# Attention values with 16 products a unit instead of 24, their halves added by an accumulating transfer

## The chip, the cores and the metric

One core of a Trainium2 chip runs the whole kernel. TensorE multiplies from the on-chip memory into eight accumulator banks (`psum`), VectorE and ScalarE read and write both, GpSimd reads and writes the on-chip memory only, and SyncE (SP) issues transfers. Each engine works through its own list in order; engines wait for one another by semaphores. The metric is the device time of one execution in microseconds (us), smaller is better, as the median over several executions.

## The reference

An adapter projection, attention, a second adapter projection and a mixture-of-experts layer over 32 sequences of 64 tokens and 1024 columns, all in 32-bit floats:

```python
x = x + attn(cond(x, labeler, W, lora_A, lora_B), w_qkv, b_qkv, w_o, b_o)
x = x + ffn(cond2(x, language, W, Wr, A, B), W_base, b_base, W_router, A, B)
...
q, k = apply_rope(q, 0), apply_rope(k, 0)          # 32 query heads, 8 key/value heads of 32
scores = where(causal, q @ k.T / sqrt(32), -1e20)
out = softmax(scores) @ v
```

## The kernel before

The kernel has five stages, one behind the other on every engine: it folds the first projection into the query/key/value weights, runs attention, folds the second projection into the last weights, then the output projection, then the mixture of experts. Precision is kept by splitting each operand into a rounded high part and a low rest and adding three products, high by high, high by low and low by high.

Attention goes over 16 units of 128 tokens, two sequences (`b` = 0, 1) each. It is a pipeline of steps over `u`, written out by hand (`steps`): a step projects unit `u`, does the scores and the softmax of unit `v = u - 1`, and the values of unit `w = u - 2`. Steps 2 to 14 are one loop body, step 15 is the same body written out; steps 0 and 1 have no values yet, step 16 has scores and values but no projection (there TensorE does the first products of the next fold, `fold2.first(k)`, in its place), and step 17 has only the last values (`last_values`).

TensorE's order within a step is set by the table `BESIDE`. The projection of a unit is cut into 8 slices `k` of 3 parts each (L912), and `(k, part): [...]` names the work that stands ahead of that part. That work is: `transpose_p` (L959), the transposition of the probabilities of one `b`; `attend` (L974), the value products of one `b`; `transpose_qk` (L931), the transposition of rotated queries and keys in three turns; `scores` (L944). At the end of the step stand the transposition of the adapter's small product (`transpose_down`, L985) and the four products `up` (L991) that finish the projection. `BESIDE_FIRST` is the table of step 1.

In `attend` the contraction runs over two heads by 64 keys, so the values stand in blocks on a diagonal: `vb_h` and `vb_l` are 128 rows by 4 x 32 columns of which half are zero. For each `b` there are 3 pairs (`vb_h` by `pt_h`, `vb_l` by `pt_h`, `vb_h` by `pt_l`) by 2 quads by 2 halves `j`, 12 products of 256 moving columns, all into the bank `s_ps[:, b]`.

VectorE per step: the low part of the probabilities (`probs_low`, L749), four multiplications of the rotation (`rotate`, L744), the low part of the values (L797), the low parts of queries and keys (L753, L816), `less_max` for each `b` (mask L834, maximum L836, subtraction L838), `inverse` (L771), `low_down` (L778), `sum_up` (L764), the low part of `lows` (L856) for which `up` waits, and the read-out of the projection (L867). ScalarE takes the high parts, reads out the values (`values_out`, L605), and forms the exponentials (L617 for `b` = 0 in 16 pieces with their sums, L619 for `b` = 1). GpSimd does the two additions of the rotation (L711, L713), the low parts of x (`split_x`, L694) and the division by the sum (`normalise`, L704). SP loads x and adapter rows and stores each unit's values into a scratch tensor (L562).

## Time and profile before

| | |
|---|---|
| median of 3 executions | 1154.16 us (1153.38 to 1154.23) |
| the profiled execution, its time | 1153.42 us |
| its span, first to last instruction | 1151.3 us |
| TensorE busy in the span | 1132.6 us, 98% |
| VectorE, ScalarE, GpSimd busy | 684.9, 409.2 and 202.8 us |
| share of TensorE in the chain that ended last | 87% |
| share of VectorE and ScalarE in that chain | 7% and 4% |

The span is what the hardware profiler saw; the execution's own time has 2.1 us more around it. Busy time of an engine is the union of its instructions; matmuls are pipelined, so a busy TensorE need not be at its peak. The chain that ended last is followed back from the last instruction, at each step to what released it.

### The profile page before, as it was taken

The numbers are of one execution on the slowest core, as the hardware profiler recorded it, in microseconds if no ns is written. First come the engines' busy times: TensorE is split into PE (matmuls) and PEld (weight loads), VectorE is DVE, ScalarE is ACT, GpSimd is POOL, SyncE is SP. The second block draws the span as 40 slices with busy tenths as digits, with TensorE's granted clock in tenths as the row PEclk, the third lists the DMA queues.
The fourth block names the chain that finished last, engine by engine and source line by source line (L and its number), as shares of the span: only waits on it lengthen the run. The fifth ranks groups of instructions, "written<-read, shape, count | busy, mean of one in ns | idle before, by whom it ended". The sixth has DMA issues, their size and how long they took to land.

```text
span 1151.3 us, 16982 instructions
## 1 busy us (share of the span) xinstructions
PE 1132.6 (98%) x6176; PEld 992.3 (86%) x6176; DVE 684.9 (59%) x1201; ACT 409.2 (36%) x1172; POOL 202.8 (18%) x131
## 2 busy tenths in 40 slices
PE   8999999999999999999989999999999999999998
PEld 6888888999999999999889998888888888888887
DVE  5312137878887888888894234233136766666664
ACT  5312124555555555555553234111123322222221
POOL 0000124443334433334351001000000000000000
PEclk9999999999999999999999999999999999999999
DMA  8020032111111111110042115473561323332222
GB/s 287 18 66 19 10 113 73 46 46 52 58 46 46 46 54 46 46 46 36 19 169 92 57 38 165 128 217 101 158 183 43 123 110 110 111 110 96 75 69 92
DMA packets 90082, 98.29 MB, mean 85 GB/s; under 512 B 7730, under 2 KB 74162, under 8 KB 90034
## 3 DMA queue, kind: packets, MB, share of 16 engines
q1 hardware_dynamic: 89890, 97.37, 26.2%
q8 instruction: 32, 0.52, 0.2%
q10 hardware_dynamic: 144, 0.26, 0.1%
q14 instruction: 16, 0.13, 0.0%
HBM read 72.45 MB, written 25.17 MB: 85 GB/s over the span
## 4 chain that ended last, share of the span: by engine, by line
PE 87%; DVE 7%; ACT 4%; DMA 1%; issue 0%; POOL 0%; DVEq 0%; SPq 0%
PE psum L912 18%; PE psum L1563 15%; PE psum L1871 14%; PE psum L280 13%; PE psum L1291 8%; PE psum L1851 4%; PE psum L974 4%; PE psum L1949 4%; ACT prob L617 3%; PE psum L944 3%; PE psum L959 2%; PE psum L931 1%; PE psum L991 1%; DVE prob L838 1%; DVE smax L836 1%; DVE prob L834 1%
## 5 line engine op out<-in xcount | busy, mean ns | idle before, releaser
L912 PE MATMUL psum<-p_h,c_high_low 128*128 128x512 f32 (+1 forms) x768 | 194.3, 360 | 0.5 <-DVE qkv L867 0.5
L912 PEld LDWEIGHTS psum<-p_h,c_high_low 128*128 128x128 f32 x768 | 133.2, 188 | 14.2 <-issue 0.7
L280 PE MATMUL psum<-c_high_low,w_h 128*128 128x512 f32 x384 | 119.5, 396 | 5.7 <-ACT c_high_low L215 5.7
L1563 PE MATMUL psum<-ring,rows 128*128 128x512 f32 x528 | 123.7, 392 | 1.0 <-DVE t_plain L1265 0.8
L1563 PEld LDWEIGHTS psum<-ring,rows 128*128 128x128 f32 x528 | 98.8, 188 | 23.9 <-DVE t_plain L1265 2.3
L1291 PE MATMUL psum<-chunk,rows 128*128 128x384 f32 (+1 forms) x576 | 108.7, 343 | 1.2 <-DVE qkv L867 0.7
L912 PE MATMUL psum<-p_l,c_high_low 128*128 128x512 f32 (+1 forms) x384 | 104.2, 366 | 0.0
L1291 PEld LDWEIGHTS psum<-chunk,rows 128*128 128x128 f32 x576 | 101.8, 190 | 2.0 <-DVE qkv L867 1.0
L280 PEld LDWEIGHTS psum<-c_high_low,w_h 128*128 128x128 f32 x384 | 73.4, 191 | 22.4 <-ACT c_high_low L215 5.7
L704 POOL TENSOR_TENSOR prob<-prob,sinv 128x1024 f32<-128x1024 f32 x32 | 61.1, 1908 | 126.7 <-DVE sinv L771 126.7
L694 POOL TENSOR_TENSOR c_high_low<-ring_plain,c_high_low 128x512 fp32r<-128x512 f32 x32 | 41.4, 1293 | 235.0 <-PE psum L280 139.1
L617 ACT ACTIVATE prob<-prob 128x64 f32<-128x64 f32 x240 | 57.8, 242 | 67.7 <-DVE prob L838 67.7
L912 PE MATMUL psum<-end_h,c_high_low 128*128 128x320 f32 x256 | 75.9, 309 | 0.0
L280 PE MATMUL psum<-c_high_low,w_l 128*128 128x512 f32 x192 | 73.9, 391 | 0.0
L912 PEld LDWEIGHTS psum<-p_l,c_high_low 128*128 128x128 f32 x384 | 66.0, 189 | 6.3
L1871 PE MATMUL psum<-t_high,s_blocks 128*128 128x512 f32 x192 | 64.6, 398 | 0.0
L266 DVE TENSOR_TENSOR p_l<-psum,p_h 128x512 fp32r<-128x512 f32 (+1 forms) x24 | 14.2, 602 | 83.1 <-ACT p_h L254 42.3
L1523 DVE TENSOR_TENSOR ring<-ring_plain,ring 128x512 fp32r<-128x512 f32 x22 | 15.2, 691 | 75.3 <-ACT ring L1518 75.3
L1563 PE MATMUL psum<-at,rows 128*128 128x512 f32 x240 | 56.5, 391 | 0.0
L912 PEld LDWEIGHTS psum<-end_h,c_high_low 128*128 128x128 f32 x256 | 47.5, 188 | 7.9
L1563 PEld LDWEIGHTS psum<-at,rows 128*128 128x128 f32 x240 | 45.0, 188 | 9.9
L1851 PE MATMUL psum<-gates,a_blocks 128*128 128x272 f32 x384 | 50.3, 290 | 0.0
(172 smaller groups left out, 2225.1 us busy)
## 6 DMA issues: line engine op xcount, KB each, us to landing
ring_plain<-in_x_t SPq DMA_DIRECT2D x32, 256.0 KB, 2.6
attn_scratch<-ring_plain SPq DMA_DIRECT2D x16, 512.0 KB, 2.6
ring_plain<-attn_scratch SPq DMA_DIRECT2D x32, 256.0 KB, 4.0
raw<-x_t_scratch SPq DMA_DIRECT2D x16, 512.0 KB, 4.1
rest<-in_b_base SPq DMA_DIRECT2D x16, 512.0 KB, 4.2
out<-rest SPq DMA_DIRECT2D x15, 512.0 KB, 2.7
ring_plain<-in_wqkv_t SPq DMA_DIRECT2D x10, 512.0 KB, 6.1
a_raw<-in_lora_a SPq DMA_DIRECT2D x32, 128.0 KB, 2.1
```

What stands on the lines that cost most here:

```text
L280: mm = pe.matmul(to, stationary, moving, start=k == 0 and m == 0, stop=k == KT - 1 and last, skip_group_check=True)
L617: last = act.activation(prob[:, 0, g, c, :], prob[:, 0, g, c, :], ACT.Exp, scale=SCALE, accum_out=ssum[:, 0, g, c:c + 1])
L694: pool.tensor_tensor(x_l[:, ks(half), :], x_raw[:, ks(half), :], x_h[:, ks(half), :].bitcast(F32), ALU.subtract).then_inc(x_low, 1)
L704: pool.tensor_tensor(rows, rows, sinv[:, b, :, :].rearrange("p g c -> p (g c)").unsqueeze(2).to_broadcast([P, 2 * KVH, SEQ]), ALU.mult).th ...
L912: mm = pe.matmul(to, sx[:, kk, :], moving(w, n, kk), start=first, stop=False, skip_group_check=True)
L944: mm = pe.matmul(o, qq[:, b, cols, :].rearrange("p g t -> p (g t)"), kk[:, q, b, :, :].rearrange("p c t -> p (c t)"), start=n == 0, stop=n ...
L974: mm = pe.matmul(s_ps[:, b, q * 4 * SEQ:(q + 1) * 4 * SEQ], vv[:, b, q, j, :, :].rearrange("p c d -> p (c d)"), pp[:, q, j, :, :].rearrang ...
L1291: mm = pe.matmul(self.tile(n, width), stationary, moving, start=k == 0 and m == 0, stop=k == KT - 1 and m == 2, skip_group_check=True)
L1563: mm = pe.matmul(self.psum[:, self.BANK_OF[i], :], w[:, cols], s, start=m == 0 and p == 0, stop=m == KT - 1 and p == 2, skip_group_check=True)
L1851: mm = pe.matmul(self.gate_ps[:, u, :], s[:, k % HALF, :], self.room.gates[:, m, k, :], start=k == 0 and n == 0, stop=k == KT - 1 and n == ...
L1871: mm = pe.matmul(self.banks[self.BANK_OF[name]], s[:, k, :], w[:, k, :], start=name in ("p1", "p5", "p6") and k == 0 and n == 0, stop=k == ...
L1949: mm = pe.matmul(self.banks[{"c11": "a", "c12": "c", "c21": "b", "c22": "d"}[name]], self.zt[:, r, s, u, :], w[m], start=name == "c22" and ...
```

## The change

Five things change. First, high and low values stand side by side in one tensor `vb`, each as 2 x 32 columns; one product with 128 stationary columns gives high by high in the upper 64 rows of the result and low by high in the lower 64, and the product with the low probabilities has 64 stationary columns. That is 8 products for each `b` in place of 12. A result of one `b` is now twice as large and lies in two banks (by quad, no longer by `b`), so the second `attend` waits until ScalarE has read out the first (`pv_out`), and ScalarE reads out in two copies each time.

Second, the upper and lower 64 rows have to be added. They lie on different partitions; GpSimd issues two transfers a unit that add the lower rows onto the upper (`add_low_values`), behind `split_x` of the first half and ahead of `normalise`. SP waits for both (`pv_summed`) and stores two halves.

Third, GpSimd's rotation waits for all four multiplications (`rot_re` and `rot_im`) before its first addition. Fourth, VectorE's low part of the values moves behind `probs_low` of the second `b`. Fifth, entries of `BESIDE` move: the transpositions of queries and keys from (2, 1) and (3, 1) to (3, 0) and (3, 2), the scores from (4, 0) and (5, 0) to (4, 2) and (5, 2). At the end of attention SP's loads for the next fold are arranged around the later last store.

```diff
-    vb_h, vb_l = (sb(n, [P, BPU, QUADS, 2, 4, HD], F32R) for n in ("vb_h", "vb_l"))
+    vb = sb("vb", [P, BPU, QUADS, 2, 2, 2, HD], F32R)
+    values = ring[:, 2, :], sb("values_odd", [P, D])
...
+            if value and not score:
+                sp.wait_ge(s_done, 2 * UNITS)
+                fold2.load_lora(sp)
+                sp.wait_ge(fold2.row_low, fold2.STAGED)
+                fold2.load_chunk(sp, 1, 0)
             if value:
-                sp.wait_ge(pv_out, 2 * w + 2)
-                sp.dma_start(a["attn"][bass.ds(w, 1), :, :].rearrange("o p c -> (o p) c"),
-                             attn[:, :, :, :].rearrange("p k b t -> p (k b t)")).then_inc(stored, 16)
+                sp.wait_ge(pv_summed, 32 * w + 32)
+                for j in range(2):
+                    sp.dma_start(a["attn"][bass.ds(w, 1), j * SEQ:(j + 1) * SEQ, :].rearrange("o p c -> (o p) c"),
+                                 values[j][high_rows, :]).then_inc(stored, 16)
...
             if b == 0:
-                need(act, stored, 16 * w)
-            act.activation(attn[:, :, b, :], s_ps[:, b, :].rearrange("p (k t) -> p k t", k=KT), ACT.Copy).then_inc(pv_out, 1)
+                need(act, stored, 32 * w)
+            for j in range(2):
+                to = values[j].rearrange("p (k b t) -> p k b t", k=KT, b=BPU)[:, :, b, :].rearrange("p (q g) t -> p q g t", q=QUADS)
+                cols = s_ps[:, :, j * GRP * SEQ:(j + 1) * GRP * SEQ].rearrange("p q (g t) -> p q g t", g=GRP)
+                last = act.activation(to, cols, ACT.Copy)
+            last.then_inc(pv_out, 1)
...
+        def add_low_values():
+            for j in range(2):
+                pool.dma_start(values[j][high_rows, :], values[j][low_rows, :], accum_op=ALU.add).then_inc(pv_summed, 16)
+
...
                 pool.wait_ge(rot_re, v + 1)
+                pool.wait_ge(rot_im, v + 1)
                 pool.tensor_tensor(roped[:, :, :, 0], roped[:, :, :, 0], rot_t[:, 0, :, :], ALU.subtract).then_inc(rotated, 1)
-                pool.wait_ge(rot_im, v + 1)
                 pool.tensor_tensor(roped[:, :, :, 1], roped[:, :, :, 1], rot_t[:, 1, :, :], ALU.add).then_inc(rotated, 1)
+            if value:
+                pool.wait_ge(pv_out, 2 * w + 2)
...
+            if value:
+                add_low_values()
             if score:
                 normalise(v, 0)
...
-            n = 0
-            for vv, pp in ((vb_h, pt_h), (vb_l, pt_h), (vb_h, pt_l)):
+            else:
+                pe.wait_ge(pv_out, 2 * v + 1)
+            for parts, pp in ((2, pt_h), (1, pt_l)):
...
-                        mm = pe.matmul(s_ps[:, b, q * 4 * SEQ:(q + 1) * 4 * SEQ], vv[:, b, q, j, :, :].rearrange("p c d -> p (c d)"),
-                                       pp[:, q, j, :, :].rearrange("p g t -> p (g t)"), start=n == 0, stop=pp is pt_l and j == 1, skip_group_check=True)
-                        n += 1
+                        v_at = vb[:, b, q, j, 0:parts, :, :].rearrange("p m h d -> p (m h d)")
+                        mm = pe.matmul(s_ps[0:parts * SEQ, q, j * GRP * SEQ:(j + 1) * GRP * SEQ], v_at, pp[:, q, j, :, :].rearrange("p g t -> p (g t)"),
+                                       start=parts == 2 and j == 0, stop=parts == 1 and j == 1, skip_group_check=True)
...
-                  (2, 1): [(attend, 2, 1), (transpose_qk, 1, (0, 1))], (3, 1): [(transpose_qk, 1, (2,))],
-                  (4, 0): [(scores, 1, 0)], (5, 0): [(scores, 1, 1)]}
+                  (2, 1): [(attend, 2, 1)], (3, 0): [(transpose_qk, 1, (0, 1))], (3, 2): [(transpose_qk, 1, (2,))],
+                  (4, 2): [(scores, 1, 0)], (5, 2): [(scores, 1, 1)]}
```

TensorE, loop body, from the second `attend` to the first turns of `transpose_qk`. Each row is a line, an operation, output and inputs and the shape; `x3` is three of a kind. Before:

```order
L974 MATMUL psum<-pt_h,vb_h 128x256 [waits pt_high]
L974 MATMUL psum<-pt_h,vb_h 128x256 x3
L974 MATMUL psum<-pt_h,vb_l 128x256 x4
L974 MATMUL psum<-pt_l,vb_h 128x256 [waits pt_low]
L974 MATMUL psum<-pt_l,vb_h 128x256 x3
L931 MATMUL psum<-ident,roped 128x128 [waits pt_low,rotated]
L931 MATMUL psum<-ident,roped 128x128 x7
L912 MATMUL psum<-p_l,c_high_low 128x512 x2
L912 MATMUL psum<-p_l,c_high_low 128x256
L912 MATMUL psum<-end_l,c_high_low 128x320
L912 MATMUL psum<-p_h,c_high_low 128x512 x2
```

The same place in the changed kernel, where `attend` is L995, the projection L931 and `transpose_qk` L950:

```order
L995 MATMUL psum<-pt_h,vb 128x256 [waits pv_out,pt_high]
L995 MATMUL psum<-pt_h,vb 128x256 x3
L995 MATMUL psum<-pt_l,vb 64x256 [waits pt_low]
L995 MATMUL psum<-pt_l,vb 64x256 x3
L931 MATMUL psum<-p_l,c_high_low 128x512 x2
L931 MATMUL psum<-p_l,c_high_low 128x256
L931 MATMUL psum<-end_l,c_high_low 128x320
L931 MATMUL psum<-p_h,c_high_low 128x512 x2
L931 MATMUL psum<-p_h,c_high_low 128x256
L931 MATMUL psum<-end_h,c_high_low 128x320
L950 MATMUL psum<-ident,roped 128x128 [waits pt_low,rotated]
```

The second `attend` has 8 products for 12, waits for `pv_out`, and is followed by two parts of the projection before the eight transpositions, which followed it at once.

TensorE, loop body, ahead of the first score product (L944). Before, from the last transposition of `transpose_qk` to the scores:

```order
L931 MATMUL psum<-ident,roped 128x128
L912 MATMUL psum<-p_l,c_high_low 128x512 x2
L912 MATMUL psum<-p_l,c_high_low 128x256
L912 MATMUL psum<-end_l,c_high_low 128x320
L912 MATMUL psum<-p_h,c_high_low 128x512 x2
L912 MATMUL psum<-p_h,c_high_low 128x256
L912 MATMUL psum<-end_h,c_high_low 128x320
L944 MATMUL psum<-k_h,q_h 128x256 [waits pv_out,k_low,qk_low]
```

In the changed kernel, where the scores are L963:

```order
L950 MATMUL psum<-ident,roped 128x128
L931 MATMUL psum<-p_h,c_high_low 128x512 x2
L931 MATMUL psum<-p_h,c_high_low 128x256
L931 MATMUL psum<-end_h,c_high_low 128x320
L931 MATMUL psum<-p_h,c_high_low 128x512 [waits x_low]
L931 MATMUL psum<-p_h,c_high_low 128x512
L931 MATMUL psum<-p_h,c_high_low 128x256
L931 MATMUL psum<-end_h,c_high_low 128x320
L931 MATMUL psum<-p_l,c_high_low 128x512 x2
L931 MATMUL psum<-p_l,c_high_low 128x256
L931 MATMUL psum<-end_l,c_high_low 128x320
L963 MATMUL psum<-k_h,q_h 128x256 [waits pv_out,k_low,qk_low]
```

Between the third turn and the scores there stood two parts of the projection (a part is one product each for the columns 2 x 512, 256 and 320), now three. Ahead of the third turn stood three behind the first two turns, now two, and two more stand ahead of these. So five parts lay between the second `attend` and the scores, and now seven.

GpSimd, loop body. Before:

```order
L711 TENSOR_TENSOR roped<-roped,rot_t 128x640 [waits rot_re]
L713 TENSOR_TENSOR roped<-roped,rot_t 128x640 [waits rot_im]
L694 TENSOR_TENSOR c_high_low<-ring_plain,c_high_low 128x512 [waits x_high]
L704 TENSOR_TENSOR prob<-prob,sinv 128x1024 [waits s_inv]
L698 TENSOR_TENSOR end_l<-a_raw,end_h 128x2x8x32 [waits a_high]
L694 TENSOR_TENSOR c_high_low<-ring_plain,c_high_low 128x512 [waits x_high]
```

In the changed kernel (`split_x` L705, the transfers L720, `normalise` L715):

```order
L727 TENSOR_TENSOR roped<-roped,rot_t 128x640 [waits rot_im,rot_re]
L728 TENSOR_TENSOR roped<-roped,rot_t 128x640
L730 ISA
L704 ISA [waits pv_out]
L705 TENSOR_TENSOR c_high_low<-ring_plain,c_high_low 128x512 [waits x_high]
L720 DMA ring_plain<-ring_plain 64x1024
L720 DMA values_odd<-values_odd 64x1024
L713 ISA
L715 TENSOR_TENSOR prob<-prob,sinv 128x1024 [waits s_inv]
```

The rotation's first addition waits for both multiplication pairs, and two transfers stand between `split_x` and `normalise`.

## Rows read from the trace of the kernel before

**Rows 1.** Windows, one loop step: length, busy PE PEld DVE ACT POOL, clock, DMA.

```profile
439.40:466.60 27.20, 27.15 (x177) 24.67 (x176) 22.44 (x34) 14.64 (x54) 11.36 (x8) 1.00 0.14 48
```

**Rows 2.** Chain that ended last, 438 to 468 us: start, us, what.

```profile
442.61 1.43 PE psum L974 x12
...
447.83 1.50 PE psum L974 x12
...
450.21 2.19 PE psum L912 x12
...
454.07 1.45 PE psum L944 x12
...
459.31 3.95 ACT prob L617 x32
```

**Rows 3.** Weight-load queue, timeline of the same step: start, us.

```profile
464.25 0.14 PEld L985 LDWEIGHTS psum<-ident,low 128*128 128x128 f32 x1
...
465.84 0.77 PEld L991 LDWEIGHTS psum<-pb,lows 128*128 128x128 f32 x4 [0.37 <-DVE lows L856]
```

**Rows 4.** Waits over the whole run: us, times, longest.

```profile
PEld psum L991 <- DVE lows L856: 5.6, 15, 0.5
```

**Rows 5.** TensorE, timeline of the same step.

```profile
439.39 1.04 PE L959 MATMUL psum<-ident,prob 128*128 128x128 f32 x8
...
449.17 1.04 PE L931 MATMUL psum<-ident,roped 128*128 128x128 f32 x8
...
453.90 0.28 PE L944 MATMUL psum<-k_h,q_h 128*128 128x256 f32 x1
...
457.53 0.27 PE L944 MATMUL psum<-k_h,q_h 128*128 128x256 f32 x1
...
466.64 0.60 PE L959 MATMUL psum<-ident,prob 128*128 128x128 f32 x4
```

**Rows 6.** VectorE, timeline of the same step.

```profile
444.13 0.82 DVE L744 TENSOR_TENSOR roped<-qkv,sin 128x640 f32<-128x640 f32 x1
444.87 2.21 DVE L744 TENSOR_TENSOR rot_t<-qkv,cos 128x640 f32<-128x640 f32 x1
...
453.24 0.41 DVE L753 TENSOR_TENSOR q_l<-psum,q_h 128x256 fp32r<-128x256 f32 x1
...
455.54 1.23 DVE L834 TENSOR_TENSOR prob<-psum,hidden 128x1024 f32<-128x1024 f32 x1 [1.06 <-PE psum L944]
...
463.46 0.59 DVE L778 TENSOR_SCALAR low<-psum 64x128 f32<-64x128 f32 x2
464.24 1.22 DVE L764 TENSOR_REDUCE ssum<-prob 128x16 f32<-128x1024 f32 x1 [0.19 <-ACT prob L619]
465.50 0.29 DVE L856 TENSOR_TENSOR lows<-psum,lows 32x128 fp32r<-32x128 f32 x1
```

**Rows 7.** ScalarE, timeline of the same step.

```profile
449.37 0.60 ACT L605 ACTIVATE ring_plain<-psum 128x512 f32<-128x512 f32 x1 [3.40 <-PE psum L974]
449.87 0.38 ACT L648 ACTIVATE keys<-psum 128x256 f32<-128x256 f32 x1
```

**Rows 8.** GpSimd, timeline of the same step.

```profile
454.93 1.29 POOL L694 TENSOR_TENSOR c_high_low<-ring_plain,c_high_low 128x512 fp32r<-128x512 f32 x1 [6.05 <-ACT c_high_low L582]
463.62 1.91 POOL L704 TENSOR_TENSOR prob<-prob,sinv 128x1024 f32<-128x1024 f32 x1 [7.41 <-DVE sinv L771]
```

**Rows 9.** Transfers to the scratch: issue and landing.

```profile
L562 SPq DMA_DIRECT2D attn_scratch<-ring_plain x16: 344/355/374, 204.8 to 618.5; - x16
...
DMA to landing us min/median/max: 2.6/2.9/6.3
```

**Rows 10.** TensorE, timeline of the last scoring step.

```profile
587.33 1.04 PE L931 MATMUL psum<-ident,roped 128*128 128x128 f32 x8
588.22 2.40 PE L1291 MATMUL psum<-chunk,rows 128*128 128x392 f32 x12
...
606.28 1.21 PE L959 MATMUL psum<-ident,prob 128*128 128x128 f32 x8 [2.01 <-POOL prob L704]
```

40 lines of the change are left out of this document (18 added, 22 removed).

## The prediction

> **What bounds the kernel now.** I read the windows of one step of the attention loop first. Of 27.20 us TensorE is busy 27.15, at full granted clock [rows 1]. That reads as a stage bound by TensorE, in which every product taken away is time won. The chain that ended last says otherwise. In each step it leaves TensorE after the score products and runs over VectorE and ScalarE: 3.95 us of it are the exponentials of the first batch [rows 2]. The weight-load queue shows where that chain comes back: the load ahead of the `up` products stood idle 0.37 us for L856 [rows 3]. The reader is to see that this happens in every step, 15 times and 5.6 us in all [rows 4]. So two limits lie 0.37 us apart: TensorE's own work, 27.25 - 0.37 = 26.88 us a step, and a loop through the softmax.
>
> I take the step's zero at its first transposition, 439.39; the next one begins at 466.64, so the step is 27.25 us. The first score product starts at 453.90, which is 14.51 after zero, and the next step begins 12.74 us after that [rows 5]. The second number is the length of the tail, and it is fixed by data: scores end, L834 starts at 455.54, three operations a batch, ScalarE's exponentials from 459.31 [rows 2], then `low_down` (L778) at 463.46, the sum L764 at 464.24, which waited for ScalarE's second exponential, and L856 at 465.50 [rows 6]. L856 lets `up` go, and `up` ends the step. TensorE's order is fixed, so the first number is pure TensorE work ahead of the scores. A step costs "TensorE work ahead of the scores" + 12.74, or TensorE's whole work, whichever is more.
>
> **The change, part by part.**
> *Products.* 24 become 16. The two groups of 12 take 1.43 and 1.50 us [rows 2], 0.119 a product, and the extra 0.07 of the second is a pause ahead of its third group for `pt_low`, which the new order on VectorE brings earlier. Eight of the new products have 64 stationary columns instead of 128. No row shows such a product. All keep 256 moving columns; the nearest row is the score products with 256 moving columns, 12 in 1.45 us, 0.121 each [rows 2]. Bounds: 0.12 and nothing. I take 0.12, because the two kinds of product in the chain with 256 moving columns cost the same. Then a group is 8 x 0.119 = 0.95, and a step's work falls by 1.43 + 1.50 - 1.90 = 1.03 us. All of it lies ahead of the scores.
> *The table.* The order above shows that the scores now stand behind two more parts of the projection. Three parts, 12 products, take 2.19 us [rows 2], so 0.73 each, and the gap from first to second scores agrees: 457.53 - 453.90 = 3.63 [rows 5], less 1.45 for the scores, is 2.18 for three. Two parts are 1.46. The first score product starts at 14.51 - 1.03 + 1.46 = 14.94.
> *Are its inputs ready by then?* The transpositions of queries and keys started at 449.17, 9.78 [rows 5], and now stand at 9.78 - 1.03 + 1.46 = 10.21. The last of the data the scores need is L753, done at 453.24 + 0.41, which is 4.48 after those transpositions [rows 6]. That gives 14.69, before 14.94. ScalarE's two copies of the values, instead of one, add one more copy of 0.50 (from 449.37 to 449.87 [rows 7]) at about 9.5; ScalarE is free again at about 10.0 and the keys are due at 10.8, so this is covered by 0.8. GpSimd's rotation starts after all four multiplications. The fourth took 2.21 us beside 0.82 for the third, since GpSimd's first rotation ran [rows 6]; now all four take 0.74 each (the distance from the start of the third, 444.13, to that of the fourth, so the first starts at 3.3) and end at 6.2. GpSimd's split of 512 columns takes 1.29 [rows 8], a rotation of 640 so some 1.6, and two end at 9.4, before 10.21. What is won, 1.4 us of VectorE, lies where VectorE waits anyway: zero. If this cover fails, each 0.1 us late is 0.1 a step.
> *Tail.* Neither VectorE's order behind the scores nor ScalarE's is touched, so 12.74 stays. `low_down` ends at 463.46 + 0.59 = 24.66 now and 25.09 then, while TensorE comes to the transposition that needs it (464.25, 24.86 now [rows 3]) at 23.83. It waits 1.3 us there, and some 0.5 at `up`. The step is 14.94 + 12.74 = 27.68 us: 0.43 longer, although it holds 1.03 us less work.
> *The accumulating transfers.* Two are issued on GpSimd behind the split of the first half, which ends at 454.93 + 1.29 = 16.83 and ahead of `normalise`, due at 463.62 (24.23) now [rows 8] and 24.66 then. So 7.8 us are free for two issues, and 1.1 more until the next step's transposition. The trace has no transfer issued by GpSimd. Bounds for one issue: SP's 0.35 us [rows 9] below, and above, for want of any such row, what the cover and the slack hold, 4.45. I take it as hidden. The Trainium skill (SBUF — State Buffer, section "A bandwidth-pool intuition that's wrong (but worth ruling out)") says a transfer issued from GpSimd that takes some 0.62 us alone takes 3.1 beside a VectorE copy that holds the shared port; two of these would be 6.2, an estimate, and still inside the cover. No row here shows it. The landing, 2.9 us for a store now [rows 9], comes twice in series, add and store, so 5.8 us behind the issue; even from 24.7 that ends at 30.5, and the next reading-out of values, which waits for it, is due at 27.7 + 4.2. SP waits for the add in front of its store, and behind that queues the load of x for the step after next, which is not read within the next 17 us.
> *Second reading-out.* The second group now waits for ScalarE to empty the banks. The first group ended at 442.61 + 1.43 = 444.04 [rows 2], 4.65, and ends at 4.2 then; two copies of 0.5 and the passing of the signals bring it to 5.5; the second group started at 447.83, 8.44, and starts at 7.9: covered by 2.4.
> *Count.* The loop and the step unrolled behind it are steps 2 to 15, 14 in all: 14 x 0.43 = +6.0. Steps 0 and 1 have no value products and their own table, untouched.
> *The last scoring step* has no projection. There the transpositions (587.33) moved behind the 12 fold products that follow them (588.22, 2.24 without the pipelined end), and the third turn has no cover left [rows 10]. If VectorE's other work absorbs it all the loss is 0; if it is passed on whole, it is some 3.3 us of later scores. TensorE waits 2.01 us for `normalise` at 606.28 [rows 10], so the chain is tight and I pass on 2.3. The two last groups save 1.0. Net +1.3, ends -1 and +4.
>
> Sum: 1153.42 (span 1151.3 + 2.1 around it) + 6.0 + 1.3 = 1160.7. The median of before is 0.7 above its profiled execution; I say 1161, 0.6% slower. An error of 0.2 us in the 14.94 is 2.8 us, so its own range is 1157 to 1166.
>
> **Rivals.**
> *A. TensorE is the bound after all, faster.* 27.15 of 27.20 busy speaks for it. Then 16 x 1.03 = 16.5 us go and the time is 1153.4 - 16.5 + 1.3 = 1138. It needs a tail shorter than 12.74 - 0.43 = 12.31 before anything is won, and under 10.9 for all. Against: the wait of [rows 4] is there in every step, and no operation of the tail is stretched by GpSimd.
> *B. The narrow products are cheap, no change.* If eight of them cost half, 0.06, the scores start at 14.47 and the step is 27.21: 1153.4 - 0.6 + 1.3 = 1154. From 0.04 downwards it would be faster. Against: the price follows the moving columns in both rows I have. The Trainium skill (TensorE: Matmul & The Clock Gate, section "LDWEIGHTS (loading the stationary operand)") has the load go with its columns, 107 ns for 128 and 53 for 64; were the load what spaces these products, 0.053 each would be about this case, an estimate. The trace cannot say which side spaces them.
> *C. GpSimd's issues gate `normalise`, slower still.* At 5 us each they run 10 - 8.9 = 1.1 us over a step, 14 x 1.1 = 15 more: 1176. It decides from 4.45 us each. For it: no row bounds such an issue from above. Against: nothing else is on GpSimd in that stretch [rows 8], and its next work starts 7.4 us behind the split.
>
> **How the numbers follow.** Forecast 0.72, A 0.10, B 0.08, C 0.10. A measurement of this kernel can tell 0.2%, 2.3 us. Slower is forecast and C, 0.82; same is B, 0.08; faster is A, 0.10. The range 1155 to 1170 holds the forecast, the upper part of B and the lower part of C, and leaves A out.
>
> **What would show it.** Right: a step of 27.7 us; TensorE idle some 1.3 us at the `low` transposition behind VectorE's `low_down` and 0.5 at `up`; 16 products a step at 0.12; score products 14.9 after the step's first transposition; `normalise` still let go by `sinv`. Wrong: a step of 26 us (A), narrow products under 0.06 (B), `normalise` behind a long issue (C), or scores that wait for `q_l`, which would lengthen the step further.

## The result, and the profile after

The changed kernel takes 1163.04 us in the median of 4 runs (1161.78 to 1163.94), the kernel before 1154.15 beside it: 8.9 us more, ratio 1.0079 with a 95% interval of 1.0067 to 1.009. Forecast were 1161 and a range of 1155 to 1170.

The profiled execution took 1163.2 us, its span is 1161.4. From the page, the busy time of each engine:

```profile
PE 1120.1 (96%) x6048; PEld 975.4 (84%) x6048; DVE 670.8 (58%) x1201; ACT 422.4 (36%) x1204; POOL 218.1 (19%) x162
```

TensorE is busy 12.5 us less than before, and the kernel ends later: where TensorE had products to do, it now waits. Windows of one loop step, as [rows 1]:

```profile
443.80:471.40 27.60, 26.29 (x169) 23.57 (x168) 21.56 (x34) 15.49 (x56) 12.40 (x10) 1.00 0.30 67
```

Of 27.60 us TensorE is now idle 1.3, where it was idle 0.05. Its timeline, as [rows 5], says where:

```profile
441.33 0.30 PE L1005 MATMUL psum<-ident,low 128*128 128x128 f32 x1 [1.13 <-DVE low L796]
...
442.97 0.96 PE L1011 MATMUL psum<-pb,lows 128*128 128x512 f32 x4 [0.18 <-DVE lows L875]
443.77 1.03 PE L978 MATMUL psum<-ident,prob 128*128 128x128 f32 x8
...
446.83 0.64 PE L995 MATMUL psum<-pt_h,vb 128*128 128x256 f32 x4
447.31 0.63 PE L995 MATMUL psum<-pt_l,vb 128*64 128x256 f32 x4
447.78 1.03 PE L978 MATMUL psum<-ident,prob 128*128 128x128 f32 x8
...
453.95 1.03 PE L950 MATMUL psum<-ident,roped 128*128 128x128 f32 x8
...
458.70 0.28 PE L963 MATMUL psum<-k_h,q_h 128*128 128x256 f32 x1
...
471.44 1.03 PE L978 MATMUL psum<-ident,prob 128*128 128x128 f32 x8
```

The step begins at 443.77; the first score product comes 14.93 us later (14.51 before, 14.94 forecast). The next step begins at 471.44, which is 12.74 after that. The first exponentials of two steps, in ScalarE's timeline, lie 27.67 apart.

```profile
436.45 0.26 ACT L628 ACTIVATE prob<-prob 128x64 f32<-128x64 f32 x1 [4.73 <-DVE prob L857]
...
464.12 0.26 ACT L628 ACTIVATE prob<-prob 128x64 f32<-128x64 f32 x1 [4.73 <-DVE prob L857]
```

The forecast was 27.68. A value group (the products of one `attend`) goes from 446.83 to 447.78, 0.95 us for eight products; its four narrow ones take 0.47 as its four wide ones do. The waits over the whole run show that both idle pieces come 15 times. The lines of PE are TensorE's own, that of PEld is the weight-load queue's, as in [rows 4]:

```profile
PE psum L1005 <- DVE low L796: 17.6, 15, 1.8
...
PEld psum L1011 <- DVE lows L875: 7.5, 15, 0.6
...
PE psum L1011 <- DVE lows L875: 2.8, 15, 0.2
```

GpSimd's timeline shows the rotation that waits for all four multiplications, the two transfers, and what `normalise` waits for:

```profile
450.21 1.60 POOL L727 TENSOR_TENSOR roped<-roped,rot_t 128x640 f32<-128x640 f32 x1 [3.20 <-DVE rot_t L762]
451.76 1.77 POOL L728 TENSOR_TENSOR roped<-roped,rot_t 128x640 f32<-128x640 f32 x1
...
460.70 0.82 POOL L720 DMA_DIRECT2D ring_plain<-ring_plain  x1
461.27 1.09 POOL L720 DMA_DIRECT2D values_odd<-values_odd  x1
468.43 1.90 POOL L715 TENSOR_TENSOR prob<-prob,sinv 128x1024 f32<-128x1024 f32 x1 [6.07 <-DVE sinv L789]
```

An issue takes 0.82 or 1.09 us, and 6 us of idle time follow them. The rotation is done at 453.53, 0.4 before the transpositions at 453.95.

### The profile page after: what moved, and what is told of

Its sections match the earlier page's. It is cut to its first block, busy times and chain, and to the rows that moved or that the text cites. A ratio compares the mean times of both kernels' runs of the same rounds, so it can differ in the third digit from the quotient of the medians.

```text
span 1161.4 us, 16875 instructions
## 1 busy us (share of the span) xinstructions
PE 1120.1 (96%) x6048; PEld 975.4 (84%) x6048; DVE 670.8 (58%) x1201; ACT 422.4 (36%) x1204; POOL 218.1 (19%) x162
## 4 chain that ended last, share of the span: by engine, by line
PE 82%; DVE 10%; ACT 7%; DMA 1%; issue 0%; POOL 0%; DVEq 0%; SPq 0%
PE psum L931 15%; PE psum L1580 15%; PE psum L1888 13%; PE psum L280 12%; PE psum L1311 8%; ACT prob L628 5%; PE psum L1868 4%; PE psum L1966 4%; PE psum L995 2%; PE psum L978 2%; PE psum L963 2%; DVE ssum L782 2%; DVE prob L857 2%; DVE smax L855 2%; DVE prob L853 2%; PE psum L950 1%
## 5 line engine op out<-in xcount | busy, mean ns | idle before, releaser
L931 PE MATMUL psum<-p_h,c_high_low 128*128 128x512 f32 (+1 forms) x768 | 196.3, 363 | 0.5 <-DVE qkv L886 0.5
L931 PEld LDWEIGHTS psum<-p_h,c_high_low 128*128 128x128 f32 x768 | 132.0, 189 | 14.6 <-issue 0.7
L931 PE MATMUL psum<-p_l,c_high_low 128*128 128x512 f32 (+1 forms) x384 | 102.1, 361 | 0.0
L705 POOL TENSOR_TENSOR c_high_low<-ring_plain,c_high_low 128x512 fp32r<-128x512 f32 x32 | 41.4, 1293 | 235.1 <-PE psum L280 139.7
L715 POOL TENSOR_TENSOR prob<-prob,sinv 128x1024 f32<-128x1024 f32 x32 | 60.9, 1902 | 99.5 <-DVE sinv L789 99.5
L931 PE MATMUL psum<-end_h,c_high_low 128*128 128x320 f32 x256 | 76.1, 309 | 0.0
L931 PEld LDWEIGHTS psum<-p_l,c_high_low 128*128 128x128 f32 x384 | 67.2, 190 | 6.3
L771 DVE TENSOR_TENSOR q_l<-psum,q_h 128x256 fp32r<-128x256 f32 (+1 forms) x48 | 24.5, 511 | 53.4 <-ACT q_h L606 52.3
L931 PEld LDWEIGHTS psum<-end_h,c_high_low 128*128 128x128 f32 x256 | 47.4, 188 | 7.8
```

The lines of the kernel that those rows point to most:

```text
L705: pool.tensor_tensor(x_l[:, ks(half), :], x_raw[:, ks(half), :], x_h[:, ks(half), :].bitcast(F32), ALU.subtract).then_inc(x_low, 1)
L715: pool.tensor_tensor(rows, rows, sinv[:, b, :, :].rearrange("p g c -> p (g c)").unsqueeze(2).to_broadcast([P, 2 * KVH, SEQ]), ALU.mult).th ...
L771: dve.tensor_tensor(q_l[:, :, n0:n1, :].rearrange("p b n t -> p n b t"), q_ps(turn, at, n1 - n0), q_h[:, :, n0:n1, :].bitcast(F32).rearran ...
L931: mm = pe.matmul(to, sx[:, kk, :], moving(w, n, kk), start=first, stop=False, skip_group_check=True)
```

## The experiments

The steps turned out to be a ring: each turn begins with an instruction that waits for the end of the turn before. The table gives its three pieces in each trace: from VectorE's read-out of the projection (L867 before, L886 after) to the first transposition of rotated queries, from there to the first score product, from there to the next read-out. All are differences of starts in the timelines of one step. Each ratio is to the kernel before as it ran beside that kernel (medians from 1153.58 to 1154.15 us).

| kernel | read-out to transposition | to scores | to next read-out | step | median, us | ratio to before, interval |
|---|---|---|---|---|---|---|
| before | 10.05 | 4.73 | 12.48 | 27.26 | | |
| changed | 10.45 | 4.75 | 12.47 | 27.67 | 1163.04 | 1.0079, 1.0067 to 1.009 |
| e1 old table | 10.06 | 4.80 | 12.47 | 27.33 | 1155.3 | 1.0014, 1.0004 to 1.0024 |
| e2 before, table alone | 11.54 | 4.76 | 12.46 | 28.76 | 1176.54 | 1.0195, 1.0178 to 1.0212 |
| e3 no addition | 10.45 | 4.76 | 12.46 | 27.67 | 1163.37 | 1.008, 1.0063 to 1.0096 |
| e4 tail | 10.22 | 4.79 | 12.34 | 27.35 | 1157.89 | 1.004, 1.0026 to 1.0055 |
| e5 last table | 10.44 | 4.76 | 12.46 | 27.66 | 1159.96 | 1.005, 1.0033 to 1.0067 |
| e6 before, tail | 10.17 | 4.73 | 12.93 | 27.83 | 1161.46 | 1.0068, 1.0051 to 1.0085 |
| e7 early and tail | 10.18 | 4.54 | 13.02 | 27.74 | 1161.35 | 1.0067, 1.0051 to 1.0084 |
| e8 rotation early | 10.50 | 4.48 | 13.03 | 28.01 | 1164.16 | 1.0089, 1.0072 to 1.0106 |
| e9 one part | 10.07 | 4.54 | 12.55 | 27.16 | 1153.0 | 0.9991, 0.9982 to 1.0 |
| e10 before, wait alone | 9.97 | 4.80 | 12.46 | 27.23 | 1152.77 | 0.9991, 0.9982 to 1.0 |
| e11 split rotation | 10.81 | 5.03 | 12.56 | 28.40 | 1169.26 | 1.013, 1.0115 to 1.0146 |
| e12 low v early | 9.96 | 4.53 | 12.57 | 27.06 | 1151.93 | 0.9985, 0.9976 to 0.9994 |

**Which part costs.** e1 gives the changed kernel the old table back, e2 gives the kernel before the new table and nothing else, e3 takes the accumulating transfers out.

```diff
-                  (2, 1): [(attend, 2, 1)], (3, 0): [(transpose_qk, 1, (0, 1))], (3, 2): [(transpose_qk, 1, (2,))],
-                  (4, 2): [(scores, 1, 0)], (5, 2): [(scores, 1, 1)]}
+                  (2, 1): [(attend, 2, 1), (transpose_qk, 1, (0, 1))], (3, 1): [(transpose_qk, 1, (2,))],
+                  (4, 0): [(scores, 1, 0)], (5, 0): [(scores, 1, 1)]}
```

That is e1; e2 is the same the other way round. e3:

```diff
-                sp.wait_ge(pv_summed, 32 * w + 32)
+                sp.wait_ge(pv_out, 2 * w + 2)
...
-            if value:
-                add_low_values()
```

> The changed kernel with the table BESIDE of before; products, reading-out, transfers and rotation stay changed. Theory (the step is TensorE's order ahead of the scores + 12.74 us): the transpositions of queries and keys now stand 8.75 us after the step's start but their input, GpSimd's rotation, is done at 9.76 (451.76 + 1.77 in the trace of the changed kernel, step start 443.77), so TensorE waits 1.0 us for it; from there to the scores 4.73 us as before, so scores at 14.5 and a step of 27.3 against 27.67: 14 x 0.4 = 5.6 us less than the changed kernel, plus 2 to 3 us in the last scoring step, so about 1155. Rival (the longer step comes from the doubled reading-out, the transfers or the rotation, not from the table): no change against the changed kernel, 1163, or slower by the added wait, 1177.

> The kernel of before with only the table moved: 24 products, no transfers. TensorE has the same work in another order. Theory: each of the two parts that now stand ahead of the scores adds its 0.73 us to every step from 2 to 15, so scores at 15.97, a step of 28.71, 14 x 1.46 = 20.4 us more, and some 3 to 5 us in the last scoring step: 1154 + 24 = 1178. Rival (TensorE's total work is the bound, order does not matter): 1154 to 1156.

> The changed kernel without the two accumulating transfers (the addition of the lower to the upper rows is left out) and with SP's stores let go by ScalarE's reading-out. Theory: the transfers lie beside waits of GpSimd and cost nothing in the loop; at the end of attention they may hold the last division by 0 to 1 us. So 1162 to 1163.5, no change that can be told, and a step of 27.67. Rival (they slow VectorE or GpSimd in the tail): 5 us or more less, and a tail under 12.74.

The moved table alone costs 22.8 us on the kernel before. Its step is 28.76, where 14.51 + 1.46 + 12.74 = 28.71 follows from the forecast's terms. Taken out of the changed kernel it gives 7.7 us back, and what is left of the change costs 1.6 us (1155.3 beside 1153.73). The transfers cost nothing that can be told: 1163.37 with no addition. But with the old table TensorE's order would have put the scores at 13.48, and they came at 14.59. The timeline of e1 names what took the products' place:

```profile
450.26 1.09 PE L950 MATMUL psum<-ident,roped 128*128 128x128 f32 x8 [0.91 <-POOL roped L728]
```

So the products taken away give no time there: the transpositions now wait for GpSimd's rotation. GpSimd's timeline of the kernel before has the second addition at

```profile
447.16 1.72 POOL L713 TENSOR_TENSOR roped<-roped,rot_t 128x640 f32<-128x640 f32 x1 [0.76 <-DVE rot_t L744]
```

The rotation was done at 448.88 there and the transpositions started at 449.17 [rows 5], so at most 0.3 us a step could be had. Rotation, low parts, scores, softmax and read-out follow each other in a ring. With the old table TensorE's product count is hardly a part of it. With the moved table it is, because the transpositions then stand behind so much of TensorE's work that they no longer wait for the rotation: the first piece is 11.54 with 24 products (e2) and 10.45 with 16.

e10 does the third part of the change alone, the wait for both pairs of multiplications:

```diff
                 pool.wait_ge(rot_re, v + 1)
+                pool.wait_ge(rot_im, v + 1)
                 pool.tensor_tensor(roped[:, :, :, 0], roped[:, :, :, 0], rot_t[:, 0, :, :], ALU.subtract).then_inc(rotated, 1)
-                pool.wait_ge(rot_im, v + 1)
```

> The kernel before, and GpSimd's first addition waits for all four multiplications: the third part of the change alone. No work is left out. Theory: the fourth multiplication is no longer stretched (2.21 to 0.82 us), but both additions now stand behind it, so that the rotation is done 10.0 us behind the read-out of the projection instead of 9.74; the transpositions, which had 0.3 us to spare, start 0.0 to 0.3 us later, a step 27.25 to 27.5, a time 1154 to 1157.5; I take 1155. Rival: VectorE's earlier end is what counts (the low part of the second probabilities comes 0.5 us earlier), and the time falls to 1151.

It costs nothing (0.9991, and the interval reaches 1), and its time lies between what the theory and the rival gave. e10 and e1 have the same table and the same wait on GpSimd, one with 24 products and one with 16, and their steps are 27.23 and 27.33; e1 also has the doubled reading-out, the transfers and the later low part of the values. From the timelines of VectorE and GpSimd in e10:

```profile
445.06 0.82 DVE L744 TENSOR_TENSOR rot_t<-qkv,cos 128x640 f32<-128x640 f32 x1
```

```profile
446.02 1.65 POOL L712 TENSOR_TENSOR roped<-roped,rot_t 128x640 f32<-128x640 f32 x1 [3.13 <-DVE rot_t L744]
447.63 1.59 POOL L713 TENSOR_TENSOR roped<-roped,rot_t 128x640 f32<-128x640 f32 x1
```

The fourth multiplication takes 0.82 us where it took 2.21 [rows 6], GpSimd's first addition 1.65 (2.11 in the kernel before). It starts 1.5 us later behind the read-out (6.71 for 5.17), and the rotation ends only 0.15 later: 449.22 less the read-out's 439.31 is 9.91, against 9.76 before.

**The tail.** In the changed kernel TensorE waits 1.13 us for `low_down`. e4 puts it ahead of the inverse of b = 0, and the low part of `lows` ahead of the sum of b = 1; e6 does the same to the kernel before.

```diff
                 if main:
                     less_max(1)
+                    low_down(u)
                     inverse(v, 0, True)
...
-            if score and main:
-                sum_up(v, 1)
             if main:
                 dve.wait_ge(low_high, u + 1)
                 rows = slice(2 * LR, 3 * LR)
                 dve.tensor_tensor(lows[rows, :], low_ps[rows, :], lows[rows, :].bitcast(F32), ALU.subtract).then_inc(low_ready, 1)
             if score and main:
+                sum_up(v, 1)
                 inverse(v, 1)
```

> The changed kernel with three operations moved on VectorE: low_down ahead of the first inverse, the low part of lows ahead of the second sum. TensorE's list is untouched. Theory: the tail binds. low_down then ends at 468.33 instead of 468.85 in the trace of the changed kernel, the low transposition follows at 468.5 and the six products behind it end at 469.95, so up goes at 469.95 instead of 470.64: tail 12.05, step 26.98, 14 x 0.69 = 9.7 us less than the changed kernel, about 1153.4. Rival (what lengthens the step lies ahead of the scores only, or in TensorE's work): 1163, no change.

> The kernel before with VectorE's order changed at the end of a step: low_down ahead of the inverse of b = 0, and the low part of lows ahead of the sum of b = 1. No work is left out. Theory: the kernel before, too, is bound by the part ahead of the scores and the tail, with a cover of some 0.3 us on TensorE; its step goes from 27.25 to no less than TensorE's own 26.9, 14 x 0.36 = 5 us, about 1149. Rival 1: its step is TensorE's work already, and the reordering gives nothing, 1154. Rival 2: GpSimd's chain behind normalise binds at once, as in the changed kernel with this reordering, and gives half, 1151 to 1152.

e4 gained half of what I expected, and e6 lost 7.6 us where I expected a gain or nothing. `up` starts 0.96 us earlier behind the scores in e4 (10.97 for 11.93), but the sum and the second inverse now stand between `lows` and the read-out of the projection, and the read-out opens the ring's next turn, so its third piece falls by 0.13 only. VectorE's timeline of e6:

```profile
440.08 0.59 DVE L778 TENSOR_SCALAR low<-psum 64x128 f32<-64x128 f32 x2 [0.46 <-PE psum L912]
...
441.67 0.29 DVE L855 TENSOR_TENSOR lows<-psum,lows 32x128 fp32r<-32x128 f32 x1 [0.72 <-ACT lows L677]
441.99 1.22 DVE L764 TENSOR_REDUCE ssum<-prob 128x16 f32<-128x1024 f32 x1
443.24 0.25 DVE L771 RECIPROCAL sinv<-ssum 128x16 f32<-128x16 f32 x1
443.53 1.89 DVE L867 TENSOR_TENSOR qkv<-psum,b_bc 128x512 f32<-128x512 f32 x3
445.33 1.22 DVE L749 TENSOR_TENSOR pt_l<-psum,pt_h 128x1024 fp32r<-128x1024 f32 x1
446.46 1.52 DVE L744 TENSOR_TENSOR roped<-qkv,cos 128x640 f32<-128x640 f32 x1
```

Ahead of `lows` VectorE sat idle 0.72 us, the hole in which the sum lay before [rows 6]; behind it no row shown has a wait, so the ring runs through VectorE itself there. And `low_down` waits 0.46 for TensorE's products: with the old table the scores come two parts earlier in TensorE's order, and VectorE is through with `less_max` before TensorE has done what `low_down` reads. In e4, with the moved table, it does not wait:

```profile
463.37 0.58 DVE L796 TENSOR_SCALAR low<-psum 64x128 f32<-64x128 f32 x2
```

Behind the first score product `low_down` starts at 8.93 in e4 and at 9.48 in e6 (467.91 less 458.43, one step later). That is most of the 0.59 between their third pieces, 12.34 and 12.93. In e6 the first multiplication takes 1.52 us beside GpSimd's `normalise` (445.37 to 447.30), in the kernel before it began when that had ended and took 0.81.

**The last scoring step.** e5 gives the changed kernel the old table in step 16 only.

```diff
+        BESIDE_LAST = {(0, 0): [(transpose_p, 2, 0)], (1, 0): [(attend, 2, 0), (transpose_p, 2, 1)],
+                       (2, 1): [(attend, 2, 1), (transpose_qk, 1, (0, 1))], (3, 1): [(transpose_qk, 1, (2,))],
+                       (4, 0): [(scores, 1, 0)], (5, 0): [(scores, 1, 1)]}
...
-                    for what, back, which in (BESIDE_FIRST if score and not value else BESIDE).get((k, part), []):
+                    for what, back, which in (BESIDE_FIRST if score and not value else BESIDE if main else BESIDE_LAST).get((k, part), []):
```

> The changed kernel with the old places of the transpositions and scores in the last scoring step alone (step 16, which has no projection). No work is left out. The run with the old table everywhere had a last scoring step some 3.3 us shorter than the changed kernel's. Theory: the moved table, not the new products, made that stage longer, because the transpositions stand behind fold products that wait for VectorE; then the steps stay at 27.67 us and the time falls by 3.3, to about 1159.8. Rival: the stage is longer because of the fold products' own waits and the fallen clock, whatever the order; then under 1 us is won, 1162 to 1163.

1159.96, 3.1 us below the changed kernel: the table's effect in one unlooped step. In the changed kernel the fold products of that step stand ahead of the transpositions and wait for VectorE (timeline), and the windows over the same stretch show the clock behind that wait (length, busy PE PEld DVE ACT POOL, clock, DMA):

```profile
591.35 0.68 PE L995 MATMUL psum<-pt_l,vb 128*64 128x256 f32 x4 [0.65 <-DVE pt_l L767]
594.83 3.91 PE L1311 MATMUL psum<-chunk,rows 128*128 128x392 f32 x12 [2.79 <-DVE rows L1179]
598.58 1.03 PE L950 MATMUL psum<-ident,roped 128*128 128x128 f32 x8
```

```profile
593.60:594.80 1.20, 0.00 (x0) 0.00 (x0) 1.20 (x2) 0.64 (x2) 0.49 (x2) 0.99 0.55 221
594.80:596.00 1.20, 1.17 (x4) 1.20 (x5) 1.20 (x1) 0.00 (x0) 1.20 (x2) 0.50 0.20 83
```

Twelve fold products take 3.91 us where they took 2.40 [rows 10], and behind the wait the granted clock fell to 0.50, the 1.2 GHz level. But e5 shows the same fall, and still wins:

```profile
593.40 1.25 PE L950 MATMUL psum<-ident,roped 128*128 128x128 f32 x8 [1.62 <-POOL roped L728]
594.57 3.76 PE L1314 MATMUL psum<-chunk,rows 128*128 128x392 f32 x12
598.17 0.38 PE L950 MATMUL psum<-ident,roped 128*128 128x128 f32 x2
```

What counts is the place: the transpositions start at 593.40 and not at 598.58, and the first score product at 600.54 and not at 603.06. From the step's first transposition to the one for which TensorE waits for `normalise` the traces have 30.53 us before [rows 10], 34.06 in the changed kernel, 31.08 in e5 and 30.73 in e1.

**All covers at once.** e7 puts the transpositions one part behind the second value group, the scores at their old places, has e5's last step and e4's tail, and moves TensorE's wait for the low adapter rows of x two parts back. e8 is e7 with GpSimd's first addition waiting for the first pair alone.

```diff
-                  (2, 1): [(attend, 2, 1)], (3, 0): [(transpose_qk, 1, (0, 1))], (3, 2): [(transpose_qk, 1, (2,))],
-                  (4, 2): [(scores, 1, 0)], (5, 2): [(scores, 1, 1)]}
+                  (2, 1): [(attend, 2, 1)], (2, 2): [(transpose_qk, 1, (0, 1))], (3, 1): [(transpose_qk, 1, (2,))],
+                  (4, 0): [(scores, 1, 0)], (5, 0): [(scores, 1, 1)]}
...
-            if k == 0 and part == 0:
+            if k == 0 and part == 2:
                 pe.wait_ge(a_low, u + 1)
```

e8, on top of that:

```diff
-                pool.wait_ge(rot_im, v + 1)
                 pool.tensor_tensor(roped[:, :, :, 0], roped[:, :, :, 0], rot_t[:, 0, :, :], ALU.subtract).then_inc(rotated, 1)
+                pool.wait_ge(rot_im, v + 1)
```

> The changed kernel with four edits: scores at (4, 0) and (5, 0) and the third turn at (3, 1) as before, the first two turns at (2, 2), one part of the projection behind the second attend, so that GpSimd's rotation has cover; the old table in the last scoring step; VectorE's reordering of the tail; and TensorE's wait for the low adapter rows of x moved from the first to the third part of slice 0, where they are first needed. No work is left out. Theory: the step is the order ahead of the scores (about 14.3) plus a tail of about 11.9, so 26.2 and near TensorE's own 25.9; with the last scoring step 3.3 shorter the time is about 1139 to 1141. Rival 1: GpSimd's rotation still gates the transpositions (the wait seen with the old table was 0.91) and the tail's gain stops at normalise: a step of 26.9, 1149 to 1151. Rival 2: TensorE was never limited by these waits, 1155 as with the old table.

> The run before this one, and GpSimd's first addition of the rotation waits for the first pair of multiplications only, as in the kernel before. No work is left out. Theory: the rotation ends earlier by at most the second pair of multiplications (1.6 us) but runs beside VectorE, which stretches both; the wait of the transpositions falls from some 0.3 to 0, a step 0 to 0.3 us shorter, a time 0 to 4 us less. Rival: the two engines hold each other up, VectorE's low parts come later by over 1 us, the scores wait for them, and the time is 3 to 10 us more.

Both theories fell. e7 is 21 us over its forecast. I had taken a tail of 11.9, which is e4's up to TensorE's next step. Up to there it is 12.57 in e7 (458.05 to 470.62), since the scores are back at their old places and `low_down` waits 0.46 for TensorE as in e6. And the ring goes on from the read-out, which the sum delays: the third piece is 13.02 in place of 12.47. e8 is worse than e7 by 0.27 a step and 2.8 us, near its rival: GpSimd's first addition stretches VectorE's fourth multiplication again, and the second `pt_l` behind it comes late. VectorE's, GpSimd's and TensorE's timelines of e8:

```profile
452.25 2.21 DVE L762 TENSOR_TENSOR rot_t<-qkv,cos 128x640 f32<-128x640 f32 x1
```

```profile
451.67 2.11 POOL L726 TENSOR_TENSOR roped<-roped,rot_t 128x640 f32<-128x640 f32 x1 [1.50 <-DVE rot_t L762]
454.54 1.57 POOL L728 TENSOR_TENSOR roped<-roped,rot_t 128x640 f32<-128x640 f32 x1 [0.76 <-DVE rot_t L762]
```

```profile
455.65 0.68 PE L995 MATMUL psum<-pt_l,vb 128*64 128x256 f32 x4 [0.87 <-DVE pt_l L767]
```

The rotation itself is done 9.72 behind the read-out (e7: 10.13), but the transpositions stand behind that wait in TensorE's order and start at 10.50 (e7: 10.18).

**The ring by itself.** e9 keeps only the table of e7 and e5's last step, VectorE's order is the changed kernel's. e12 is e9 with the low part of the values back ahead of the low probabilities of b = 1. e11 goes for the ring's first piece: VectorE does two multiplications, the low probabilities of b = 0, then the other two; GpSimd waits for each pair; the first value group and the second transposition of probabilities move to (1, 2).

```diff
                 rotate(v, 0)
+                if value and main:
+                    probs_low(w, 0)
                 rotate(v, 1)
```

That is e11 on VectorE; its table is the old one with the entry (1, 0) at (1, 2). e12 on VectorE, on top of e9:

```diff
                 rotate(v, 1)
+                dve.wait_ge(v_high, v + 1)
+                dve.tensor_tensor(v_hl[:, 1, :, :, :, :].rearrange("p q j h d -> p (q j h d)"), qkv[:, QK:QKV],
+                                  v_hl[:, 0, :, :, :, :].rearrange("p q j h d -> p (q j h d)").bitcast(F32), ALU.subtract).then_inc(v_low, 1)
...
             if value:
                 probs_low(w, 1)
-            if score:
-                dve.wait_ge(v_high, v + 1)
...
```

> The changed kernel with only TensorE's table edited: the first two turns of the transposition one part behind the second attend at (2, 2), the third at (3, 1), the scores at (4, 0) and (5, 0), and the old table in the last scoring step. VectorE's order is the changed kernel's. No work is left out. Theory, now a ring of waits: from the read-out of the projection to the first transposition 10.06 us (as in the run with the old table, where it waits for GpSimd's rotation), from there to the first score product 4.54 (as in the run of all edits, where the scores wait for q_l), from there to the next read-out 12.47 (as in the changed kernel and with the old table). Sum 27.07, 0.26 less than with the old table, 14 steps, 3.6 us less than 1155.3, so 1151.7. Rival: VectorE's low parts queue behind each other and the second piece is 4.8 whatever the table; then 1155.

> The changed kernel with the old table, except that the first attend and the second transposition of probabilities stand at (1, 2), and with the rotation split: VectorE does the first two multiplications, then the low part of the probabilities of b = 0, then the other two; GpSimd's first addition waits for the first two only. The last scoring step is as with the old table. No work is left out. Theory: GpSimd's first addition lies beside probs_low in place of the multiplications, and the rotation is done some 8.9 us behind the read-out instead of 10.0; the first transposition then starts where TensorE's order puts it, 9.36 behind the read-out. 9.36 + 4.80 + 12.47 = 26.63 a step, 0.70 less than with the old table, 14 steps, 9.8 us: about 1145.5. Rival 1: GpSimd stretches probs_low and the next multiplication as it stretched the fourth one before, and the rotation is done no earlier: 1155. Rival 2: the low probabilities of b = 0 now come too late for the first attend and the second transposition, and the step is longer than 27.4: over 1156.

> The kernel with one part behind the second attend, and VectorE's low part of the values ahead of the low probabilities of b = 1, as in the kernel before: the fourth part of the change undone. No work is left out. Theory: the ring of waits sets the step. GpSimd's second addition took 1.76 us where the low part of the values lies beside it and 1.59 in the kernel before with the one wait, where it does not; the ring is then 27.16 - 0.1 = 27.06 and 14 steps give 1.4 us: 1151.6, faster than both kernels. Rival: the low probabilities of b = 1 come 0.4 us later and the second attend or the first transposition, which needs them, waits as long; then the step is 27.2 to 27.5 and the time 1153 to 1157.

e9 was to have a step of 27.07 and has 27.16, because the third piece grew by 0.08: 1153.0 measured, 1151.7 expected. In TensorE's timeline of e9 the ring is tight at both places:

```profile
449.28 1.09 PE L950 MATMUL psum<-ident,roped 128*128 128x128 f32 x8 [0.20 <-POOL roped L728]
...
453.82 0.39 PE L963 MATMUL psum<-k_h,q_h 128*128 128x256 f32 x1 [0.28 <-DVE q_l L771]
454.04 0.28 PE L963 MATMUL psum<-k_l,q_h 128*128 128x256 f32 x1
454.16 0.27 PE L963 MATMUL psum<-k_h,q_l 128*128 128x256 f32 x1
```

The last rows also show where the 0.08 comes from. The first score product has waited, and the second follows it after 0.22 us and not after 0.12 as the third follows the second. In the changed kernel, where the scores do not wait, the first distance is 0.13. Counted from the fourth score product to the read-out the piece is 12.10 in e9 (454.27 to 466.37) and 12.11 in the changed kernel (459.06 to 471.17), so nothing else grew.

The products taken away pay for the part of cover in e9: they are 1.03 us of TensorE's work and the part is 0.73. With 24 products the same table would put the transpositions at about 10.05 + 0.73 = 10.78, an estimate from the row of before; that kernel was not run.

e11 failed. Its first multiplication now starts while GpSimd still does the second `normalise`, in GpSimd's timeline

```profile
450.91 1.91 POOL L715 TENSOR_TENSOR prob<-prob,sinv 128x1024 f32<-128x1024 f32 x1
```

and in VectorE's:

```profile
451.36 2.14 DVE L765 TENSOR_TENSOR roped<-qkv,cos 128x640 f32<-128x640 f32 x1 [0.22 <-DVE qkv L892]
453.42 0.81 DVE L765 TENSOR_TENSOR rot_t<-qkv,sin 128x640 f32<-128x640 f32 x1
454.16 1.21 DVE L770 TENSOR_TENSOR pt_l<-psum,pt_h 128x1024 fp32r<-128x1024 f32 x1
455.29 1.29 DVE L765 TENSOR_TENSOR roped<-qkv,sin 128x640 f32<-128x640 f32 x1
```

and TensorE waits for the late low probabilities in every step, twice (waits over the whole run):

```profile
PE psum L1001 <- DVE pt_l L770: 18.8, 30, 0.8
```

That is rival 2 of its expectation. What is stretched is not `probs_low`, as rival 1 had it, but the multiplications, 2.14 us beside `normalise` and 1.29 beside the addition. e12 came out as worked out, 27.06 a step and 1151.93 us; GpSimd's timeline has the second addition at 1.59 us for 1.77 in the changed kernel:

```profile
443.89 1.65 POOL L727 TENSOR_TENSOR roped<-roped,rot_t 128x640 f32<-128x640 f32 x1 [3.13 <-DVE rot_t L762]
445.50 1.59 POOL L728 TENSOR_TENSOR roped<-roped,rot_t 128x640 f32<-128x640 f32 x1
```

It beats both kernels, the one before by 0.15%, with an interval that excludes no change.

## Why the prediction was right, point by point

The forecast was the right case; it was 2 us short, 1161 for 1163.04.

- *The step.* Forecast 14.94 + 12.74 = 27.68, measured 14.93 + 12.74. The loop gives 14 x 0.42 = 5.9 of the 8.9 us. e2 shows the table's share by itself (28.76 for 28.71).
- *Products.* 0.95 us a group, as forecast. Rival B fell: four narrow products take 0.47 us like four wide ones, although their weight loads are shorter, 134 ns in the mean for 188.
- *Waits.* 1.3 us were expected at the `low` transposition, 1.13 came. At `up` I expected 0.5; the weight-load queue, where I had read the 0.37 of the kernel before, shows 0.5 (7.5 us in 15 waits), and TensorE 0.18.
- *Covers.* The rotation was to end 9.4 behind the step's start and ended at 9.76, still ahead of the transpositions at 10.18. I had left out the signal from VectorE to GpSimd (0.14), and took 1.6 for the second addition, which is 1.77. So half of the 0.8 us of cover was not there, and what was left sufficed.
- *Transfers.* Hidden, as forecast; e3 shows it. Rival C needed 4.45 us an issue and got 0.82 and 1.09. The rule of the Trainium skill (SBUF — State Buffer, section "A bandwidth-pool intuition that's wrong (but worth ruling out)") has 3.1 for one beside a VectorE copy; what VectorE did beside these issues was a mask and a maximum and no copy, so the rule as such was not tested, and the estimate of 6.2 that I drew from it is over three times the 1.9 measured.
- *Rival A* did not come, for one reason more than I gave. The tail was one; e1 shows that with the old table the products are held up at another place, GpSimd's rotation, and no kernel here brought the step below 27.06, whatever TensorE's work. The ring of rotation, low parts, softmax and read-out has about 27.1 us of its own; TensorE's work of the kernel before (26.9) was all but hidden in it. So the forecast's sum, TensorE's work ahead of the scores and 12.74, holds only where TensorE comes to the transpositions after the rotation. In the changed kernel it does, by 0.42 us; for e1 the same sum would give 13.48 + 12.74 = 26.22, and the step was 27.33.
- *The term that was mis-sized* is the last scoring step: net +1.3 forecast, about 3.0 measured (8.9 less 5.9). The later scores cost 3.1 (e5) for the 2.3 taken, and the 1.0 for the two shorter groups did not come: e5 is 6.1 us above the kernel before beside it, of which the loop has 5.9, so its last steps are +0.2 and not -1.0. Its rows above show the 1.62 us wait for GpSimd's rotation just behind the second group, where shorter products lengthen a wait. These sums use medians beside different runs of the kernel before (1154.15 and 1153.83); the two profiled executions put the last scoring step 3.5 us above (34.06 for 30.53). A fall of the clock, 1.5 us on twelve fold products, comes there in some traces and not in others, so the account of this step is not sharper than that.
- *What is no effect.* The first exponentials of the run start at 187.5 us, at 186.7 in the kernel before. With e3 it is 186.4, and with e10, where that stage is as before, 187.2: this is scatter of single executions.

My own forecasts behind the prediction were worse than it. e4, e6 and e7 moved the sum from ahead of `lows` to behind it, ahead of the read-out, which I did not yet count as part of the ring. e11 put off low probabilities for which TensorE waits.

Two things stay open: what of the last scoring step's 3 us belongs to which of its waits, and whether the later start of GpSimd pays by itself. e10's gain over before (0.9991) is not told from nothing.

## What to carry to other kernels

When an engine is 98% busy and still has a small wait in every step, look for the ring of dependencies of nearly the same length before taking work off the engine: measure it as the distances between the same three or four instructions in consecutive steps, and see whether the edit shortens one of them. Moving a consumer behind more work, to cover a wait, costs that work once it stands on the ring: one part of cover with the scores in place (e9) had a step of 27.16, two parts with the scores moved 27.67. Before an operation is moved into or out of an idle gap, ask what the engine will do next and whether that opens the ring's next turn: a sum of 1.22 us taken out of a gap of 0.72 was part of what cost 7.6 us, the other part being `low_down`'s wait for TensorE (e6). In a step outside the loop, a table made for the loop must be looked at by itself: 3.1 of 8.9 us came from one such step.

## What the runs showed of the hardware

- VectorE and GpSimd side by side: a VectorE multiplication of 128x640 takes 0.82 us alone and 2.21 beside GpSimd's addition of the same shape, which itself takes 2.11 for 1.65. So GpSimd may start 1.5 us later and end only 0.15 later (e10). Beside `normalise`, a GpSimd operation of 128x1024, a multiplication took 1.51 to 1.55 us (e4, e6, e7, e8) and 2.14 (e11).
- VectorE's `pt_l`, which reads an accumulator bank, took 1.21 us beside GpSimd's addition in e11 and 1.23 with GpSimd idle (changed kernel, at 618.36): it was not stretched.
- The granted clock fell to 0.50, the 1.2 GHz level, after some short pauses and not after others. After a wait of 2.79 us it fell (changed kernel), after 1.62 it fell in e5 and not in e1, where the same wait is followed by twelve fold products in 2.39 us; after 2.14 it fell in e12 (3.80 us), after 2.09 it did not in e10 (2.36). After the 2.01 us wait for `normalise` it fell in the kernel before (three fold products in 1.33 us) and not in the changed one (0.79). The length of the wait alone doesn't decide it.
- A product that has waited is followed by the next after 0.22 us, and one that has not after 0.12 (score products of 256 columns, e9).
- A product of 256 moving columns takes its 0.12 us with 128 and with 64 stationary columns alike; the weight loads took 188 and 134 ns in the mean (changed kernel).
- An accumulating transfer of 64x1024 from one half of the partitions to the other costs GpSimd 0.82 or 1.09 us to issue (medians of 16 each). The first of a pair lands after 3.5 us and the second after 5.1, medians again (3.4 to 5.4 over all).
